# The last chunk of a graph aggregation: first expert tiles beside its last twelve steps, and a tighter router for the chunk before it

## The reference, cut to what matters

```
# graph part: y = x + concat(xn, adj @ xn, edge) @ weight + bias, with xn = layernorm(x)
neighbor_node_features = adj @ node_features            # adj is 5000 x 5000
neighbor_edge_features = einsum('ij,ji->i', adj, adj)
support = concatenate((node_features, neighbor_node_features, neighbor_edge_features), axis=1)
return support @ weight + bias

# expert part: every row goes to its best 2 of 8 experts
logits = xf @ gate_w + gate_b
probs = softmax(logits)
top2_vals, top2_idx = top_k(probs, 2)
for each expert e:                                      # H = 256
    h = gelu(xf @ W1[e] + b1[e])
    acc = acc + weight_e[:, None] * (h @ W2[e] + b2[e])
out = x + acc
```

## Time and profile before

| | us |
|---|---|
| median of 3 runs | 1405.32 (1403.5 to 1409.83) |
| span of the profiled execution | 1406.8 (the page shows no other time of it) |
| chunk 9's aggregation on PE | 1204.95 to 1236.06 |
| round k = 10 and the nine early tiles on PE | 1236.06 to about 1284 |
| POOL without a pause | 1248.12 to 1382.58 |
| loading back, adding, writing out | to 1406.8 |

### The profile page before, as it was taken

How to read it: one execution, slowest core, us unless ns; L and a number is a source line. 1 busy time by engine, 2 the same in 40 slices (tenths; PEclk the granted TensorE clock), 3 DMA queues, 4 the chain that set the end, 5 groups by cost and what they waited for, 6 DMA issues and landing times.

```text
span 1406.8 us, 20911 instructions
## 1 busy us (share of the span) xinstructions
PE 1294.1 (92%) x6560; PEld 818.7 (58%) x6560; DVE 922.4 (66%) x2683; ACT 645.5 (46%) x1175; POOL 426.3 (30%) x427
## 2 busy tenths in 40 slices
PE   5899999999999999999989999999998999988950
PEld 2344445454545454554778998466666666766840
DVE  7776877777686877777542232877776777854323
ACT  3445444443434444343444554665555555543420
POOL 2102020202020202021365554302322333267772
PEclk9999999999999999999999999999999999999985
DMA  9798998889898979798559993789897988846846
GB/s 311 244 355 296 363 352 333 284 318 318 288 347 269 361 252 357 252 335 267 203 175 406 334 303 117 287 291 314 316 317 270 323 316 311 271 124 181 246 135 226
DMA packets 120974, 399.76 MB, mean 284 GB/s; under 512 B 19920, under 2 KB 51170, under 8 KB 91552
## 3 DMA queue, kind: packets, MB, share of 16 engines
q1 hardware_dynamic: 80512, 339.66, 69.1%
q10 hardware_dynamic: 28288, 34.98, 7.1%
q0 software_dynamic: 12064, 23.80, 4.6%
HBM read 346.44 MB, written 56.89 MB: 287 GB/s over the span
## 4 chain that ended last, share of the span: by engine, by line
PE 26%; DVE 11%; issue 8%; POOL 5%; DMA 2%; ACT 2%; POOLq 0%; SPq 0%; DVEq 0%; ACTq 0%
PE d L896 6%; POOL y_scratch L1882 3%; DVE adj_over_wb L398 3%; PE u L963 2%; PE agg L963 2%; PE u L880 2%; PE agg L968 1%; POOL rows_scratch L1873 1%; PE u L968 1%; PE agg L970 1%; PE agg L969 1%; PE u L970 1%; PE u L969 1%; PE u L882 1%; PE u L881 1%
## 5 line engine op out<-in xcount | busy, mean ns | idle before, releaser
L787 PE MATMUL agg<-m,xn 128*128 128x512 f32 (+1 forms) x800 | 402.8, 586 | 0.0
L1117 ACT ACTIVATE mabs<-m 128x512 f32<-128x512 f32 (+1 forms) x400 | 239.7, 617 | 309.4 <-DVE m L1635 208.6
L1635 DVE TENSOR_TENSOR m<-s,ring 128x512 f32<-128x512 f32 (+1 forms) x400 | 268.8, 675 | 149.0 <-PE s L763 128.1
L763 PE MATMUL s<-ymov,ysta 128*128 128x512 f32 (+1 forms) x400 | 263.3, 659 | 24.8 <-DVE m L1635 15.8
L1873 POOL DMA_INDIRECT rows_scratch<-xrow,idx x160 | 170.1, 1063 | 295.6 <-DVE xrow L1361 104.0
L787 PEld LDWEIGHTS agg<-m,xn 128*128 128x128 f32 x800 | 151.9, 190 | 68.5 <-issue 48.1
L1882 POOL DMA_INDIRECT y_scratch<-yo,ids x144 | 142.2, 987 | 83.5 <-issue 52.0
L763 PEld LDWEIGHTS s<-ymov,ysta 128*128 128x128 f32 x400 | 76.0, 190 | 153.7 <-issue 95.2
L398 DVE TENSOR_TENSOR adj_over_wb<-ring,adj_over_wb 128x512 fp32r<-128x512 f32 (+1 forms) x216 | 138.9, 673 | 34.5 <-ACT adj_over_wb L1220 32.1
L1220 ACT CAST adj_over_wb<-ring 128x512 fp32r<-128x512 f32 (+1 forms) x216 | 125.8, 607 | 52.4 <-PE agg L970 26.3
L1859 POOL TENSOR_TENSOR rstd<-vareps,mhalf 128x4 f32<-128x4 f32 x30 | 38.6, 1286 | 365.7 <-DVE vareps L1273 365.7
(11 more groups left out here) (278 smaller groups left out, 2270.3 us busy)
## 6 DMA issues: line engine op xcount, KB each, us to landing
ring<-in_adj_in SPq DMA_DIRECT2D x180, 1024.0 KB, 6.0
ring<-in_adj_out SPq DMA_DIRECT2D x30, 1024.0 KB, 7.8
rows_scratch<-yo ACTq DMA_DIRECT2D x81, 260.0 KB, 7.2
wb<-blob_scratch SPq DMA_DIRECT2D x24, 834.0 KB
stage<-in_adj_out SPq DMA_DIRECT2D x19, 1024.0 KB, 9.4
ring<-in_adj_in SPq DMA_DIRECT2D x20, 784.0 KB, 5.2
wb_more<-blob_scratch SPq DMA_DIRECT2D x15, 834.0 KB
xt<-rows_scratch SPq DMA_DIRECT2D x60, 130.0 KB, 4.1
```

The lines of the kernel that those rows point to most:

```text
L763: pe.matmul(sbank[s % 2][:, 0:width(k)], ysta[:, s * P:(s + 1) * P], ymov[:, k % 2, 0:width(k)], start=True, stop=True).then_inc(s_made, 1)
L787: pe.matmul(abank[:, 0:n], xn[:, b, :], m[:, b % M_BUFS, 0:n], start=b == 0, stop=b == NB - 1).then_inc(S["agg_blocks"], 1)
L1117: act.activation(mabs[:, b % ABS_BUFS, 0:width(k)], m[:, b % M_BUFS, 0:width(k)], ACT.Abs).then_inc(abs_made, 1)
L1635: dve.tensor_tensor(m[:, s % M_BUFS, 0:width(k)], sbank[s % 2][:, 0:width(k)], slot_part(LOAD_AT[k, l, False][0], s % LB, width(k)), ALU.m ...
```

## The change

The tiles run 11 steps earlier (`TILE_LEAD`): tile 0 is turned behind step 31 of chunk 9, tiles 0 and 1 and three quarters of tile 2 stand beside steps 32 to 42, and the eighth tile ends in step 20 of the round k = 10. Chunk 8's middle part, beside chunk 9's aggregation, gets a table of its own, `Z_NINTH`: its parts stand up to eight steps earlier and closer together. POOL's scatter of tile 0 moves ahead of the power of chunk 9.

```
+Z_NINTH = {"bias": 1, "edge": 2, "aux": 3, "turn_aux": 6, "copy_aux": 8, "product": 9, "aggregate": 4, "residual": 10,
+           "stats": 11, "var": 12, "power": 13, "norm": 14, "turn": 16, "copy": 17, "router": 18, "logits": 19,
+           "top": (20, 21, 22), "exp": 20, "weights": 27, "rank": 24, "place": 26, "scatter": 28}
...
+TILE_LEAD = 11
+
+
+def z_at(k):
+
+    return Z_LAST if k == CH else Z_NINTH if k == CH - 1 else Z_AT
...
     def beside(layer, s):
 
-        i, q = divmod(s, TILE_STEPS[layer])
+        i, q = divmod(s + TILE_LEAD * layer, TILE_STEPS[layer])
...
         def z_iteration(k, agg, mid):                        # on PE; on ACT, DVE and POOL likewise
-            S, n, at = SZ, width(k), Z_LAST if k == CH else Z_AT
+            S, n, at = SZ, width(k), z_at(k)
...
-                if k == CH - 1 and s == STEPS - 1:
+                if k == CH - 1 and s == STEPS - 1 - TILE_LEAD:
                     turn_in(TILES)
-                if k == CH:
-                    tile_beside(1, s)
+                if k >= CH - 1:
+                    tile_beside(1, s - (CH - k) * STEPS)
...
-                if k == CH and s in (8, 10, 14, 18):
-                    scatter_tile(TILES + (8, 10, 14, 18).index(s))
+                if k == CH and s in (0, 8, 12, 16):
+                    scatter_tile(TILES + (0, 8, 12, 16).index(s))
```

More of the change, by code:

```diff
@@ L1201, in z_iteration @@
         def z_iteration(k, agg, mid):
-            j, at = k - 1, Z_LAST if k == CH else Z_AT
+            j, at = k - 1, z_at(k)
             for s in range(STEPS):
@@ L1747, in z_iteration @@
         def z_iteration(k, agg, mid):
-            S, at = SZ, Z_LAST if k == CH else Z_AT
+            S, at = SZ, z_at(k)
             for s in range(STEPS):
@@ L1806, in z_iteration @@
                     early_table(1, s - 1)
[L1807 to L1810, removed]
+                if k >= CH - 1:
+                    tile_beside(1, s - (CH - k) * STEPS)
+                if k == CH and s == at["place"] + 1:
+                    make_table(1)
         z_pipeline(dve, z_iteration)
@@ L1911, in z_iteration @@
         def z_iteration(k, agg, mid):
-            at = Z_LAST if k == CH else Z_AT
+            at = z_at(k)
             for s in range(STEPS):
```

## The result

| | before | after |
|---|---|---|
| median | 1410.72 (20 runs, 1403.5 to 1416.88) | 1418.5 (20 runs, 1412.68 to 1426.65) |
| ratio, 95% interval | | 1.005 [1.0033, 1.0066] |
| profiled execution: time, span | not given, 1406.8 | 1414.87, 1413.1 |

The change makes the kernel slower by 7.0 us (4.7 to 9.3): 0.5% of 1410.72. The three runs of before that were known when the prediction was made had a median of 1405.32; with 20 runs it is 1410.72.

What follows compares the result with a forecast made beforehand. POOL's unbroken scatters bound the kernel before; after the change chunk 9's rows wait for the router. E +10.4 with a 28.4 us chain starts the rows 5.7 us later: span 1406.8 to 1412.5, 1411.0 on the median's scale, range 1403.5 to 1417.

Steps and rivals of the forecast that it cites:

- E: Time when PE has finished chunk 9's last aggregation block, 1236.06 before; forecast to move by +10.4 us.
- The tiles: Tile products on PE ahead of chunk 9's last block: 9.2 us, 1.2 absorbed, 0.4 new waits, net +8.4.
- The delay ahead of the first turn: PE's blocks 28 and 29 end +2.0 us later, block 28's split being queued on DVE behind chunk 8's weights.
- Power: Start of chunk 9's power on POOL: E + 10.0 before, forecast E' + 10.6, with POOL idle about 10 us.
- E': E after the change: forecast end of chunk 9's last aggregation block on PE, 1246.4.
- Weights: End of chunk 9's router chain on DVE: forecast E' + 28.4, bounds 26.5 and 31, with row scatters starting then.
- 4.5 us: Most a head start for POOL could be worth: chunk 9's row weights ended 4.5 us before POOL came.
- the 137.7 us behind them are unchanged: From chunk 9's first row scatter to the span's end, 113.5 us of scatters plus 24.2 us were claimed untouched.
- B: Rival: PE swallows the tiles, E moves by 6, the chain shrinks to 25; -0 to -2 us; chance 0.22.
- C: Rival: a stall opens in the loop and the clock falls, or DVE waits for POOL; 1414 to 1417; chance 0.25.
- The rule on ACT's table loads: Each table switch costs about 2.66 us; two ahead of a tile's gelu hold PE 2 to 3 us, span near 1415.
- D: Rival: tile rows are not there at step 31, so PE waits for them in the aggregation; chance 0.03.

Runs made afterwards that it cites:

- e1: The changed kernel without the ninth chunk's router table, tiles still 11 steps early; 1.0021 [0.9999, 1.0043] against the kernel before.
- e9: Changed kernel with tiles 2 steps early, no ninth table, tiles 0 to 4 scattered before chunk 9's rows; 0.996, again 0.9971, against the kernel before.
- e3: The changed kernel with tile 4's scatter also ahead of chunk 9's rows, in POOL's pause; 1.0021 [1.0, 1.0042] against the kernel before.
- e11: One of the profiled experiments; the text given does not say what it changed and gives no time under this name.
- e5: Changed kernel with tiles 3 steps early, no ninth table, tiles 0 to 4 scattered before chunk 9's rows; 0.9995 [0.9978, 1.0012] against the kernel before.
- e6: The changed kernel with tiles 7 steps early instead of 11 and no ninth table; 1.0015 [0.9999, 1.0032] against the kernel before.
- e7: The kernel before with the exponential of the router's weights replaced by a copy, so wrong weights; 1.0021 [1.0003, 1.0039] against the kernel before.

## Why the prediction missed

**The level, 5.4 of the 7.5 us.** The forecast was 1411.0, measured 1418.5, above the range's end of 1417. The step that failed is "That span lies 1.5 us over the median of the runs shown, 1405.3; the page gives no other time of it. On the median's scale: 1411.0." Every profiled execution with both numbers has a time 1.7 to 1.8 us over its span (1414.87 and 1413.1 after the change). By that the profiled execution of before took about 1408.6 (an estimate), and its own scale would have given 1412.5 + 1.8 = 1414.3, which is 3.3 of the 5.4 us. The other 2.1 is that three runs were a poor level and this execution a short one: 20 runs of the same kernel reach from 1403.5 to 1416.88 with a median of 1410.72, and beside the experiments its medians were 1409.88 to 1412.1. The range was made of mechanisms alone; a level from three runs that differ by 6.3 us among themselves is itself uncertain by several us, and none of that was in the range. By the forecast difference on the level of 20 runs it would have been 1410.7 + 5.7 = 1416.4, and the measured 1418.5 is 2.1 above that.

**The difference, 2.1 us.** Forecast +5.7; the medians differ by 7.8 and the ratio gives 7.0 (4.7 to 9.3), so the forecast lies inside. Step by step, from the table:

- E: forecast +10.4, measured +10.1. The tiles: 9.2 - 1.2 + 0.4 = +8.4, by e1 +8.2. The delay ahead of the first turn: +2.0, by e1 against the change 1.96. In the changed kernel 1.29 us of it is one wait for DVE (before 1226.57, above).
- Weights of chunk 8 near 1229.3 on the scale of before: 24.3 us after the first block; measured 24.2 (1226.04 - 1201.82). Right.
- Power: forecast E' + 10.6, measured 10.8. POOL's pause for it: about 10 us, measured 8.47, because POOL had also waited 2.96 us for tile 0's output, which the forecast had at nothing. That costs nothing, as POOL waits for the power anyway.
- Rank product: E' + 24.2, measured 24.6. The stall fell from 2.13 to 0.37 us and the clock was 1.00, as the windows of the changed kernel show, one from the wait of 1.29 us to the end of the loop and one over the chain (before: 0.94 over the chain, 0.63 in its worst part):

```profile
1226.00:1244.00 18.00, 17.29 (x90) 13.09 (x91) 8.89 (x20) 8.65 (x15) 11.34 (x11) 1.00 0.46 136
...
1243.70:1272.70 29.00, 27.71 (x183) 21.05 (x182) 16.33 (x65) 15.61 (x25) 14.21 (x15) 1.00 0.43 127
```

- Weights: E' + 28.4, measured 28.8.
- Mis-sized: I let POOL's row scatter start when the weights end. It starts 0.9 us later (DVE ends 1271.82, POOL 1272.73). The same gap stood in the trace of before at chunk 8's rows (1231.98 to 1232.89), where POOL also waits for the weights, and I had not looked there. It is the largest error of the difference that repeats in every profile where the rows wait, and with the 0.4 above it shifts the break-even of E from 4.6 to 3.3. The "4.5 us" that a head start could be worth at most is 3.6 by the same gap.
- Mis-sized: "the 137.7 us behind them are unchanged". The order is unchanged, as said, but POOL's 88 scatters took 116.35 us from the first row scatter instead of 113.48. 2.15 of it is scatters that took over 1.0 us, which differ from one execution to the next; the other 0.7 comes with the median tile scatter at 0.98 us instead of 0.97. The two executions of each kernel show how much of this is chance: 113.48 and 115.19 us before, 116.35 and 115.22 after. (The prediction's "1.28 each" divides by 80 where 79 gaps lie between 80 starts: they are 1.30 on the average and 1.28 by the median. Its sum for POOL hardly feels it.)

**The rivals.** B (PE swallows the tiles) fell: E moved by 10.1, and the chain got no shorter. Its sum was also wrong: 6 + 27.2 = 33.2 against today's 33.0 is no gain, not "-0 to -2 us". Its condition, though, is what e9 uses: E must move by less than 3.3. C did not come: the wait of 1.29 us in the loop was followed by a granted clock of 1.00, and between 1236 and 1273 DVE has no wait for POOL. The rule on ACT's table loads would have held PE another 2 to 3 us. ACT of the changed kernel, at chunk 9's exponential:

```profile
1261.50 0.59 ACT L1158 COPY tile_xz<-s 128x512 f32<-128x512 f32 x1 [0.53 <-PE s L871]
1262.11 1.28 ACT L1249 ACT_TABLE_LOAD   x1
1263.40 0.23 ACT L1249 ACTIVATE ex<-lg 128x32 f32<-128x32 f32 x1
1263.65 1.28 ACT L1166 ACT_TABLE_LOAD   x1
1264.94 1.26 ACT L1166 ACTIVATE h<-u,wbz 128x512 f32<-128x512 f32 x2
```

From the end of the copy to the gelu's start it is 2.85 us, the two loads and the 0.23 us of the exponential with no gap of more than 0.03, and PE's wait for it was 0.37. The Trainium skill (ScalarE: Activation LUTs, What ACT_TABLE_LOAD costs) adds a drain of about 1.38 us to each load; this trace has no room for it here on either side of a load.

D's rows were there: PE's turn of tile 0 at 1227.76 has no wait ahead of it.

The mechanism, then, was right: the head start that the tiles give POOL is lost waiting for chunk 9's power and then for its weights, because the tiles push E back by more than the slack of the chain behind it. The level and two terms at POOL were off. That the 2.1 us left of the difference is small is in part luck: the timed ratio allows anything from 4.7 to 9.3 us, and 2.15 us of the profile's +9.6 are slow scatters that came by chance.

## What to carry to other kernels

In this kernel, work pulled ahead on the engine that feeds the critical chain delayed that chain by nearly its full length (9.2 us of products by 8.2); the most that the delay may be is the slack of that chain against the queue it feeds: the time at which the queue arrives, less that at which its data are ready, less the hand-over gap (64.15 - 59.66 - 0.91 = 3.6 us by the trace of before, 3.3 by the runs). Fill a queue's new pause with work from behind it before asking for more head start (e3: 4 scatters moved, 5.3 us of stretch). And count milestones from a common early instruction before two traces are compared, take the level from many runs, and put the spread of runs in the range.

## What the runs showed of the hardware that was not expected

- A wait on the weights costs POOL 0.9 us from DVE's end to the indirect DMA's start, here and at chunk 8's rows; out of its own queue the gap is 0.30 us.
- An indirect scatter of 128 rows holds POOL 0.96 to 1.00 us and 1.28 from start to start. Some take 1.1 to 1.5 us at places that change from run to run: together 1.3 to 3.8 us over 1.0 us each, in a stretch of 84 or 88 of them. The median was 0.97 in the four profiles with the order of before on POOL and 0.98 in the other ten; why is open.
- Identical code up to chunk 9 reached it between 1201.6 and 1210.7 us, and a spread of about that size was there at the end of layer 1 (666.2 to 674.5). Two places can be read. In the first 60 us PE is busy for 39.9 (e11) to 45.0 us (after): after, e9 and e5, whose last product of layer 1 starts at 666.2, 667.5 and 669.3, have no wait over 1 us between 28 and 60 us, and the other eleven have waits of 1.7 to 3.9 us there, for DVE. And near 1080 PE waits for DVE in all of them. In the 12 us behind a wait of 3.31 us (the second execution of the kernel before, from 1076.6) the granted clock was 1.00, behind one of 3.50 us (e6, from 1082.6) it was 0.61. From the end of these waits to chunk 9's first block it is 124.9 and 128.0 us, which is 3.1 of the 9.1 us between these two executions. In each of the 16 groups of timed runs that have a clock, the time is lower where the mean granted clock is higher (correlation -0.56 to -0.90). Why the same code gets different waits and clocks is open.
- A wait of 1.29 us on PE in the loop left the granted clock of the stretch behind it at 1.00, and with the exponential gone the 2.13 us stall and the 0.94 of the chain went together (e7). By the two waits near 1080 above, the length of a wait alone does not tell what the clock does.
